# W_base stage of an AdaLN-FFN kernel: product 6 of pairs 2 to 7 as seven inner products for two pairs at once

## The chip, the cores and the metric

One core of one Trainium2 chip (trn2) runs the whole kernel. The metric is the device time of one execution in microseconds, as the median of several runs.

## The reference, cut to what matters

```python
def cond(v, q):                       # v: 16 x 512 x 1024, q: 16 x 512
    q_emb = relu(q @ W3 + b3)
    x = (n * v + sum(v, axis=1)) * q_emb[:, None, :]
    return relu(x @ W2 + b2)          # W2: 1024 x 1024

def ffn(y):
    base = y @ W_base + b_base        # W_base: 1024 x 1024
    shared = (y @ A_s) @ B_s
    gates = top2(softmax(y @ W_router + b_router))
    routed = ((y @ A_r) * gates) @ B_r
    return base + shared + routed

out = x + ffn(cond(x, cond_1024))
```

All in 32-bit floats. The two large products are `@ W2` (stage 1) and `@ W_base` (stage 2), for 16 batches of 512 tokens.

## The kernel before, in words

**Pairs and products.** The 16 batches are worked in 8 pairs, first through stage 1, then, as pairs 0 to 7 again (`g` = 8 to 15, `p = g - 8`), through stage 2. A pair is a 2 x 2 block matrix (two batches, two halves of the 1024 features) and is multiplied by the 2 x 2 blocks of the weight with seven products instead of eight (Strassen's scheme in Winograd's form). The products are numbered 0 to 6; their left operands are the four blocks and four sums of them (`t1` to `t4`). A product has four groups, one for each output tile of 128 features (`j`); a group is 4 chunks (`k`) of 128 x 3 matmuls of 128 x 512. The three stand for one exact one: an operand is split into a high part (ScalarE, `high`, to `act_hi`) and a low part (VectorE, `low`, to `act_lo`), and the helper `three` multiplies high by high, low by high and high by low. A group is 12 matmuls.

**Joined products.** Pairs 2 to 7 of stage 2 are taken two by two: an even one (`even`) and the odd one after it (`odd`). Product 1 of both, and product 4 of both, is again a 2 x 2 block product and is done by seven inner products (`inner`) of 12 matmuls each, all in the even pair. They take their weights from DRAM (`inner_scratch`) to `inner_w` through GpSimd's queue, one step ahead; their operands are `inner_high` and `inner_low` on 1024 columns, with four inner sums (`inner_t1` to `inner_t4`). The other pair's block waits in `partner` or `partner4`. Product 6 is done pair by pair at the pair's end.

**Banks.** Of the 8 PSUM banks, 0 to 3 hold a pair's running sums: product 0 writes them, products 2, 3, 5 and 6 add to them, and between two products an engine takes out what that bank holds then (`copy_p0`, `copy_u2`, `copy_u4` on ScalarE, `c12_bank`, `c22_of`, `c21` on VectorE). Banks 4 to 7 serve the inner products and the low-rank rows of C11.

**Low-rank rows.** `shared` and `routed` are a product of 128 rows (`ha`, `hb`) that is added onto the output tiles: three matmuls a tile, for C12 and C11 as tiles of their own (`low_rank_c12`, `low_rank_c11`), for the rest inside `group` of products 5 and 6.

**What sets the order.** Each engine runs a list that is written out by hand (`even`, `odd`, `before_next` for VectorE; `even`, `odd` for ScalarE and TensorE), strictly in order; semaphores tie the lists. SyncE's queue loads the inputs, intermediate y and x, and stores the outputs. `bank_free` and `inner_free` say what a group waits for before it writes its bank:

```python
                elif n == 5:
                    if four_joined(g):
                        pe.wait_ge(c12_base, base_no(g, j))
...
                else:
                    pe.wait_ge(c22_done, four(g, j))
```

**The end of a pair** is, on TensorE, product 5 (in an even pair with three inner products between its groups) and the four groups of product 6; on VectorE `before_next`: the low part of the next pair's product 0, chunk by chunk, with C21 of this pair (`c21`, line 1841 through `add_bank`) and `t1` of the next (line 1789) between them.

## Time and profile before

| | us |
|---|---|
| median of 3 runs | 1389.74 |
| lowest, highest | 1389.46, 1389.89 |
| the profiled execution's own time | 1388.26 |
| its span | 1386.5 |
| TensorE matmul (PE), weight load (PEld) busy | 1382.0, 1135.4 |
| VectorE (DVE), ScalarE (ACT), GpSimd (POOL) busy | 1037.3, 663.3, 75.2 |
| HBM read, written | 171.69 MB, 82.71 MB |

The span runs from the first to the last instruction of the profiled execution; times in rows count from its start. A matmul's row gives 389 ns, because matmuls overlap: what one costs is the distance between the starts of two. Names in a row read output<-inputs, `xN` is a count, and what stands in brackets is the idle time before the instruction and who ended it. Most lines are those of helpers: 2786 to 2788 are the three matmuls of `three`, 1773 and 2187 the low parts of 512 and 1024 columns, 1841 a bank plus bias plus buffer, 2204 and 2216 a bank plus buffer, 2463 the low-rank rows added to C11, 1789, 1816 and 1837 the sums t1, t3 and t4.

### The profile page before, as it was taken

The page shows a single profiled execution, that of the slowest core. Times are in us where ns is not written, and L with a number is a line of the kernel's source. Part 1 is how long each engine was busy: PE and PEld are TensorE (multiplying, and loading weights), DVE is VectorE, ACT ScalarE, POOL GpSimd, SP SyncE. Part 2 cuts the span into 40 slices and gives each one's busy share as a digit, 9 for nine tenths or more (in the row PEclk, how much of TensorE's full clock was granted, in tenths as well). Part 3 has the DMA queues.
Part 4 walks back from the last instruction along what each step waited for, and adds up shares of the span by engine and source line. Part 5 has one row for each costly group of instructions (what it writes and reads, how often), then busy time and mean ns, then how long its engine had stood idle before and what let it go on. Part 6 is the DMA issues. An engine that isn't in the chain of part 4 may idle for free.

```text
span 1386.5 us, 18363 instructions
## 1 busy us (share of the span) xinstructions
PE 1382.0 (100%) x6069; PEld 1135.4 (82%) x6069; DVE 1037.3 (75%) x1700; ACT 663.3 (48%) x1209; POOL 75.2 (5%) x163
## 2 busy tenths in 40 slices
PE   9999999999999999999999999999999999999999
PEld 5888888888888888888888888888888888888887
DVE  6977777675776757867889768887777876778665
ACT  7774755647556574655554233443224432344231
POOL 2000110000000000000000000110001000010000
PEclk9999999999999999999999999999999999999999
DMA  8253835545165451545836629868575684846734
GB/s 320 66 178 113 264 124 156 176 116 172 62 177 163 120 166 58 158 150 175 293 124 175 240 94 348 312 193 273 179 257 175 203 277 164 280 158 202 241 117 157
DMA packets 151327, 255.63 MB, mean 184 GB/s; under 512 B 40416, under 2 KB 40672, under 8 KB 151232
## 3 DMA queue, kind: packets, MB, share of 16 engines
q1 hardware_dynamic: 135680, 199.75, 44.6%
q0 software_dynamic: 13680, 49.81, 11.7%
q10 hardware_dynamic: 1872, 4.89, 0.9%
q8 instruction: 48, 0.79, 0.2%
q14 instruction: 47, 0.39, 0.1%
HBM read 171.69 MB, written 82.71 MB: 183 GB/s over the span
## 4 chain that ended last, share of the span: by engine, by line
PE 100%; DVE 0%; DVEq 0%; issue 0%
PE ps L2786 33%; PE ps L2787 33%; PE ps L2788 33%; PE ps L2797 1%; PE ps L2812 0%; PE ps L2806 0%; DVE buf L2779 0%; DVEq L59 0%; DVE zeros L1954 0%
## 5 line engine op out<-in xcount | busy, mean ns | idle before, releaser
L2786 PE MATMUL ps<-act_hi,w_hi 128*128 128x512 f32 x1504 | 585.3, 389 | 0.0
L2788 PE MATMUL ps<-act_hi,w_lo 128*128 128x512 f32 x1504 | 585.1, 389 | 0.0
L2787 PE MATMUL ps<-act_lo,w_hi 128*128 128x512 f32 x1504 | 585.1, 389 | 0.0
L2786 PEld LDWEIGHTS ps<-act_hi,w_hi 128*128 128x128 f32 x1504 | 282.3, 188 | 59.6 <-DVE act_lo L1766 0.9
L2788 PEld LDWEIGHTS ps<-act_hi,w_lo 128*128 128x128 f32 x1504 | 282.3, 188 | 58.7
L2787 PEld LDWEIGHTS ps<-act_lo,w_hi 128*128 128x128 f32 x1504 | 282.3, 188 | 58.6
L1011 ACT ACTIVATE act_hi<-src 128x512 fp32r<-128x512 f32 x208 | 124.8, 622 | 95.9 <-PE ps L2788 91.9
L1773 DVE TENSOR_TENSOR act_lo<-src,act_hi 128x512 fp32r<-128x512 f32 x192 | 129.3, 684 | 22.1 <-ACT act_hi L1011 22.1
L1030 ACT ACTIVATE yhi<-buf 128x512 fp32r<-128x512 f32 x128 | 80.2, 626 | 81.1 <-PE ps L2788 80.6
L1841 DVE SCALAR_TENSOR_TENSOR buf<-ps,bb_sb,buf 128x512 f32<-128x512 f32 x91 | 67.2, 746 | 56.3 <-PE ps L2788 54.0
L2786 PE MATMUL ps<-act_hi,inner_w 128*128 128x512 f32 x252 | 98.1, 389 | 0.0
L2788 PE MATMUL ps<-act_hi,inner_w 128*128 128x512 f32 x252 | 98.1, 389 | 0.0
L2787 PE MATMUL ps<-act_lo,inner_w 128*128 128x512 f32 x252 | 98.0, 389 | 0.0
L1841 DVE SCALAR_TENSOR_TENSOR buf<-ps,b_sb,buf 128x512 f32<-128x512 f32 x80 | 59.4, 748 | 43.7 <-PE ps L2788 43.6
L1766 DVE SCALAR_TENSOR_TENSOR act_lo<-src,shift,act_hi 128x512 fp32r<-128x512 f32 x104 | 76.7, 748 | 19.2 <-ACT act_hi L1008 19.2
L1011 ACT ACTIVATE act_hi<-buf 128x512 fp32r<-128x512 f32 x64 | 39.6, 628 | 79.4 <-DVE buf L1806 57.0
L1008 ACT ACTIVATE act_hi<-src,shift 128x512 fp32r<-128x512 f32 x100 | 69.9, 714 | 11.4 <-PE ps L2788 9.4
L1896 DVE TENSOR_TENSOR buf_lo<-buf,yhi 128x512 fp32r<-128x512 f32 x64 | 43.5, 687 | 35.8 <-ACT yhi L1030 35.7
L961 ACT ACTIVATE src<-src,qn 128x512 f32<-128x512 f32 x92 | 65.4, 711 | 4.7 <-DMA src<-in_xT 4.7
L1063 ACT ACTIVATE buf<-ps 128x512 f32<-128x512 f32 x60 | 35.7, 595 | 66.5 <-PE ps L2788 66.5
L1052 ACT ACTIVATE buf<-ps 128x512 f32<-128x512 f32 x64 | 37.2, 591 | 55.8 <-PE ps L2788 55.5
L1773 DVE TENSOR_TENSOR act_lo<-buf,act_hi 128x512 fp32r<-128x512 f32 x64 | 43.1, 687 | 27.3 <-ACT act_hi L1011 27.2
(181 smaller groups left out, 1659.8 us busy)
## 6 DMA issues: line engine op xcount, KB each, us to landing
src<-in_xT SPq DMA_DIRECT2D x224, 256.0 KB, 3.8
y_scratch<-buf SPq DMA_DIRECT2D x128, 256.0 KB, 3.2
src<-y_scratch SPq DMA_DIRECT2D x128, 256.0 KB, 5.3
inner_w<-inner_scratch POOLq DMA_DIRECT2D x63, 512.0 KB, 3.8
outT<-buf SPq DMA_DIRECT2D x115, 256.0 KB, 4.8
inner_scratch<-staged POOLq DMA_DIRECT2D x14, 512.0 KB, 5.1
wl_raw<-in_wbase SPq DMA_DIRECT2D x7, 1024.0 KB, 5.7
partner<-y_scratch POOLq DMA_DIRECT2D x12, 512.0 KB, 5.0
```

What stands on the lines that cost most here:

```text
L961: nc.scalar.activation(src[:, t, :], src[:, t, :], ACT.Identity, scale=qn[:, H * HALF_OF[q] + k, 2 * i + BATCH_OF[q]:2 * i + BATCH_OF[q] + 1],
L1008: nc.scalar.activation(act_hi[:, slot(g, n, k), :], source[:, t, :], ACT.Identity, bias=shift[:, t:t + 1]).then_inc(hi_done, 1)
L1011: nc.scalar.activation(act_hi[:, slot(g, n, k), :], source[:, t, :], func).then_inc(hi_done, 1)
L1030: nc.scalar.activation(yhi[:, (y_no(i, c, j) - 1) % 2, :], buf[:, j, :], func).then_inc(yhi_done, 1)
L1052: nc.scalar.activation(buf2[:, j, :], ps[:, j, :], ACT.Copy).then_inc(u2_copied, 1)
L1766: nc.vector.scalar_tensor_tensor(act_lo[:, s, :], source, shift[:, t:t + 1], act_hi[:, s, :].bitcast(F32), ALU.add, ALU.subtract).then_inc ...
L1773: nc.vector.tensor_tensor(act_lo[:, s, :], source, act_hi[:, s, :].bitcast(F32), ALU.subtract).then_inc(lo_done, 1)
L1841: nc.vector.scalar_tensor_tensor(buf, ps[:, bank, :], bias, buf, ALU.add, ALU.add).then_inc(done, 1)
L1896: nc.vector.tensor_tensor(lo, y, hi, ALU.subtract).then_inc(ylo_done, 1)
L2786: nc.tensor.matmul(out, wh, a_h, start=start, stop=False, skip_group_check=onto)
L2787: nc.tensor.matmul(out, wh, a_l, start=False, stop=False, skip_group_check=onto)
L2788: return nc.tensor.matmul(out, wl, a_h, start=False, stop=stop, skip_group_check=onto)
```

## The change

Product 6 of an even and the odd pair after it becomes seven inner products, like products 1 and 4, but in the odd pair: four stand behind the groups of product 3, three between the groups of product 5. The even pair's operand t4 is kept for them (`keep_t4`, a copy to `partner6` on ScalarE); `inner_tiles` takes the odd pair's t4 as the other. The even pair's C21 is gathered in `acc6` (bank plus bias plus buffer in `c21_of`, then three inner results in `six_add`) and stored in the odd pair. The low-rank rows of product 6 become tiles of their own (`low_rank_d`), the first before the last group of product 5, three behind it. In the first couple of pairs (2 and 3) the seven inner weights are made from a quadrant that is loaded again: seven high parts and seven stores on ScalarE, seven low parts and four sums on VectorE. `before_next` is no longer called for these pairs; low parts, C21 and t1 are written into `even` and `odd`. In `odd` the order of t3, t4 and the low parts changes.

```diff
+            def keep_t4(e):
+
+                g = QUADS[e]
+                for q in range(2):
+                    if e == EARLY:
+                        act.wait_ge(four_stored[q], 16 * four_stores(4, q))
+                    else:
+                        act.wait_ge(inner_done, inner_no(RUN[e - 1, 6], L2 - 1, 1))
+                for h in range(2):
+                    act.wait_ge(t4_made, four(g, 2 * h + 1))
+                    at = slice(tile(G21, 2 * h), tile(G21, 2 * h + 2))
+                    kept = nc.scalar.activation(partner6[:, 2 * h:2 * h + 2, :], src[:, at, :], ACT.Copy)
+                kept.then_inc(a_ready, 1)
...
+            def six_add(e, m, jt):
+
+                r, g = RUN[e, 6], QUADS[e]
+                dve.wait_ge(inner_done, inner_no(r, m, jt))
+                bank = (A_BANKS if m % 2 == 0 else B_BANKS)[jt]
+                if m in (0, 1, 2, 5):
...
+                    nc.vector.tensor_tensor(buf2[:, j, :], ps[:, bank, :], buf2[:, j, :], ALU.add
+                                            ).then_inc(inner_added, 1)
+                elif m == 3:
+                    dve.wait_ge(c21_done, four(g, 2 + jt))
+                    nc.vector.tensor_tensor(acc6[:, 2 + jt, :], ps[:, bank, :], acc6[:, 2 + jt, :], ALU.add
+                                            ).then_inc(inner_added, 1)
+                elif m == 4:
+                    dve.wait_ge(inner_added, added_no(r, SIX_V, jt))
+                    nc.vector.tensor_tensor(acc6[:, 2 + jt, :], ps[:, bank, :], acc6[:, 2 + jt, :], ALU.add
+                                            ).then_inc(c21_out, 1)
+                else:
+                    dve.wait_ge(c21_done, four(g, jt))
+                    nc.vector.tensor_tensor(acc6[:, jt, :], ps[:, bank, :], acc6[:, jt, :], ALU.add
+                                            ).then_inc(c21_out, 1)
+
+            def c21_of(p, j):
+
+                g = NP + p
+                bias = bb_sb[:, H + j:H + j + 1]
+                dve.wait_ge(lr_done, lr_no(p, LR_D, j))
+                if g in QUADS:
+                    dve.wait_ge(x21_added, four(p, H - 1))
+                    dve.wait_ge(buf2_stored[j], 16 * g)
+                    if g == SECOND:
+                        dve.wait_ge(inner_w_lo, 4 * L2)
+                    nc.vector.scalar_tensor_tensor(acc6[:, j, :], ps[:, j, :], bias, buf2[:, j, :], ALU.add, ALU.add
+                                                   ).then_inc(c21_done, 1)
+                else:
+                    f = RUN[QUADS.index(g - 1), 6]
+                    dve.wait_ge(inner_added, added_no(f, SIX_P1, j) if j < 2 else added_no(f, SIX_P6, j - 2))
+                    add_bank(j, bias, buf2[:, j, :], c21_done)
...
+                first = e == EARLY
...
+                if first:
+                    inner_weight_low(3 * L2)
...
+                if first:
+                    inner_weight_low(3 * L2 + 1)
                 inner_low(f, 3)
...
                 add_u2(f, 0)
+                if first:
+                    inner_weight_low(3 * L2 + 2)
+                    inner_weight_sums(3)
                 inner_low(f, 4)
                 low(g, 5, 0)
                 low(g, 5, 1)
...
                 add_u2(f, 1)
                 inner_low(f, 5)
                 u4_add_x(p, 0)
+                if first:
+                    inner_weight_low(3 * L2 + 3)
                 u4_add_x(p, 1)
                 inner_low(f, 6)
+                if first:
+                    inner_weight_low(3 * L2 + 4)
                 add_u4(f, 0)
                 add_u4(f, 1)
                 u4_add_x(p, 2)
                 u4_add_x(p, 3)
                 c22_of(p, 0)
+                lr_low_d(p)
+                if first:
+                    inner_weight_low(3 * L2 + 5)
                 c22_of(p, 1)
                 add_p6(f, 0)
                 add_p6(f, 1)
-                low(g, 6, 0)
-                low(g, 6, 1)
-                lr_low_d(p)
-                c22_of(p, 2)
                 u2_add_x(p, 2)
                 u2_add_x(p, 3)
-                low(g, 6, 2)
-                low(g, 6, 3)
                 u2_add_x(p, 0)
                 u2_add_x(p, 1)
+                low(g + 1, 0, 0)
+                low(g + 1, 0, 1)
+                if first:
+                    inner_weight_low(3 * L2 + 6)
+                c22_of(p, 2)
+                c21_of(p, 0)
+                low(g + 1, 0, 2)
+                low(g + 1, 0, 3)
                 c22_of(p, 3)
+                for j in range(1, H):
+                    c21_of(p, j)
+                    t1(g + 1, j - 1)
+                t1(g + 1, H - 1)
 
...
             def odd(p):
                 g = NP + p
+                e = QUADS.index(g - 1)
+                f = RUN[e, 6]
                 for j in range(H):
                     t2(g, j)
                     if j > 0:
...
                 low(g, 2, H - 1)
                 lr_low_a(p)
                 for j in range(H):
+                    t4(g, j)
                     low(g, 3, j)
-                    t3(g, j)
-                    t4(g, j)
-                    if j == 0:
-                        lr_low_b(p)
                     if j > 0:
                         c11_add_low(p, j - 1)
+                for j in range(H):
+                    t3(g, j)
+                lr_low_b(p)
+                inner_low(f, 0)
+                inner_t1(f)
                 c11_add_low(p, H - 1)
+                inner_low(f, 1)
+                inner_t2(f)
+                u2_add_x(p, 0)
+                u2_add_x(p, 1)
+                six_add(e, 0, 0)
+                six_add(e, 0, 1)
+                inner_low(f, 2)
+                inner_t3(f)
+                c12_bank(p, 0)
+                u2_add_x(p, 2)
+                u2_add_x(p, 3)
+                six_add(e, 1, 0)
+                six_add(e, 1, 1)
+                inner_low(f, 3)
+                inner_t4(f)
+                c12_bank(p, 1)
+                six_add(e, 2, 0)
+                six_add(e, 2, 1)
+                inner_low(f, 4)
+                for j in range(H):
+                    low(g, 5, j)
+                c12_bank(p, 2)
+                six_add(e, 3, 0)
+                six_add(e, 3, 1)
+                inner_low(f, 5)
+                c12_bank(p, 3)
                 for j in range(H):
                     c11_add_x(p, j)
-                    low(g, 5, j)
-                    c12_bank(p, j)
-                for j in range(H):
-                    u4_add_x(p, j)
-                    u2_add_x(p, j)
-                for j in range(H):
-                    low(g, 6, j)
-                    if j == 2:
-                        lr_low_d(p)
+                six_add(e, 4, 0)
+                six_add(e, 4, 1)
+                inner_low(f, 6)
+                u4_add_x(p, 0)
+                u4_add_x(p, 1)
+                lr_low_d(p)
+                c22_of(p, 0)
+                u4_add_x(p, 2)
+                u4_add_x(p, 3)
+                c22_of(p, 1)
+                six_add(e, 5, 0)
+                six_add(e, 5, 1)
+                for j in range(H):
                     c12_add_x(p, j)
-                    if j > 0:
-                        c22_of(p, j - 1)
-                c22_of(p, H - 1)
+                c22_of(p, 2)
+                if p < LAST:
+                    low(g + 1, 0, 0)
+                    low(g + 1, 0, 1)
+                c21_of(p, 0)
+                six_add(e, 6, 0)
+                six_add(e, 6, 1)
+                if p < LAST:
+                    low(g + 1, 0, 2)
+                    low(g + 1, 0, 3)
+                c22_of(p, 3)
+                c21_of(p, 1)
+                c21_of(p, 2)
+                if p < LAST:
+                    t1(g + 1, 0)
+                    c21_of(p, 3)
+                    for j in range(1, H):
+                        t1(g + 1, j)
 
...
-                    if n == 4 or 0 < e < EARLY:
+                    if n == 6:
+                        pe.wait_ge(c11_low, low_no(g + 1 - NP, 2 + jt))
...
+            def low_rank_d(p, j):
+
+                pe.wait_ge(c22_done, four(NP + p, j))
+                if j == 0:
+                    pe.wait_ge(lr_lo_done, 3 * p + 4)
+                cols = slice((H + j) * P, (H + j + 1) * P)
+                three(ps[:, j, :], low_hi[:, cols], low_lo[:, cols], ha_hi[:, :], ha_lo[:, :], False, True,
+                      True).then_inc(lr_done, 1)
+
+            def last_part(g, f):
+                for j in range(H):
+                    group(g, 5, j, (1, 3 * (g - NP) + 3, hb_hi, hb_lo))
+                    if j < H - 1:
+                        inner(f, H + j)
+                    if j == H - 2:
+                        low_rank_d(g - NP, 0)
+                for j in range(1, H):
+                    low_rank_d(g - NP, j)
+
             def even(e):
                 g = QUADS[e]
                 r, f = RUN[e, 1], RUN[e, 4]
...
                 for j in range(H):
                     group(g, 3, j)
                     inner(f, j)
-                for j in range(H):
-                    group(g, 5, j, (1, 3 * (g - NP) + 3, hb_hi, hb_lo))
-                    if j < H - 1:
-                        inner(f, H + j)
+                last_part(g, f)
 
             def odd(p):
                 g = NP + p
+                f = RUN[QUADS.index(g - 1), 6]
                 for j in range(H):
                     group(g, 0, j)
                 for j in range(H):
                     group(g, 2, j)
                     low_rank_c11(p, j)
-                group(g, 3, 0)
-                group(g, 3, 1)
-                low_rank_c12(p, 0)
-                group(g, 3, 2)
-                low_rank_c12(p, 1)
-                group(g, 3, 3)
-                low_rank_c12(p, 2)
-                low_rank_c12(p, 3)
-                for j in range(H):
-                    group(g, 5, j, (1, 3 * p + 3, hb_hi, hb_lo))
+                for j in range(H):
+                    group(g, 3, j)
+                    if j > 0:
+                        low_rank_c12(p, j - 1)
+                    inner(f, j)
+                low_rank_c12(p, H - 1)
+                last_part(g, f)
```

VectorE at the border from an odd pair to an even one (pair 3 to pair 4), before: the low parts of the next product 0 (1773), the four additions that end C21 (1841 into buf2) and t1 (1789), then the first inner low part (2187) and the first inner sum of the even pair.

```order
L1773 TENSOR_TENSOR act_lo<-src,act_hi 128x512
L1841 SCALAR_TENSOR_TENSOR buf2<-ps,bb_sb,buf2 128x512
L1789 TENSOR_TENSOR src<-src 128x512
L1773 TENSOR_TENSOR act_lo<-src,act_hi 128x512
L1841 SCALAR_TENSOR_TENSOR buf2<-ps,bb_sb,buf2 128x512
L1789 TENSOR_TENSOR src<-src 128x512
L1773 TENSOR_TENSOR act_lo<-src,act_hi 128x512
L1841 SCALAR_TENSOR_TENSOR buf2<-ps,bb_sb,buf2 128x512
L1789 TENSOR_TENSOR src<-src 128x512
L1841 SCALAR_TENSOR_TENSOR buf2<-ps,bb_sb,buf2 128x512
L2187 TENSOR_TENSOR act_lo<-src,act_hi 128x1024
L2121 SCALAR_TENSOR_TENSOR partner<-partner,src 128x1024
```

The same place now (1898 was 1773, 1966 was 1841, 1914 was 1789, 2322 was 2187, 2251 was 2121; 2395 is `six_add`).

```order
L1966 SCALAR_TENSOR_TENSOR buf3<-ps,bb_sb,buf3 128x512
L1898 TENSOR_TENSOR act_lo<-src,act_hi 128x512 x2
L1966 SCALAR_TENSOR_TENSOR buf2<-ps,bb_sb,buf2 128x512
L2395 TENSOR_TENSOR acc6<-ps,acc6 128x512 x2
L1898 TENSOR_TENSOR act_lo<-src,act_hi 128x512 x2
L1966 SCALAR_TENSOR_TENSOR buf3<-ps,bb_sb,buf3 128x512
L1966 SCALAR_TENSOR_TENSOR buf2<-ps,bb_sb,buf2 128x512 x2
L1914 TENSOR_TENSOR src<-src 128x512
L1966 SCALAR_TENSOR_TENSOR buf2<-ps,bb_sb,buf2 128x512
L1914 TENSOR_TENSOR src<-src 128x512 x3
L2322 TENSOR_TENSOR act_lo<-src,act_hi 128x1024
L2251 SCALAR_TENSOR_TENSOR partner<-partner,src 128x1024
```

Three t1 now stand together between the last C21 and the first inner low part, and the last C22 (into buf3) stands just before the C21 additions.

VectorE in the even pair 2, between the third inner product's result and the low parts of product 5, before (2216 is the bank addition, 2187 the fifth inner low part, 1773 x4 product 5's):

```order
L2167 SCALAR_TENSOR_TENSOR t2_four<-src,t2_four 128x1024
L1841 SCALAR_TENSOR_TENSOR acc4<-ps,bb_sb,acc4 128x512
L2216 TENSOR_TENSOR acc4<-ps,acc4 128x512
L2187 TENSOR_TENSOR act_lo<-partner4,act_hi 128x1024
L1773 TENSOR_TENSOR act_lo<-src,act_hi 128x512 x4
```

And now:

```order
L2302 SCALAR_TENSOR_TENSOR t2_four<-src,t2_four 128x1024
L1966 SCALAR_TENSOR_TENSOR acc4<-ps,bb_sb,acc4 128x512
L2351 TENSOR_TENSOR acc4<-ps,acc4 128x512
L2186 TENSOR_TENSOR staged_6<-wl_raw,staged_6 128x512
L2204 TENSOR_TENSOR wl_raw<-wl_raw 128x2x256
L2205 TENSOR_TENSOR wl_raw<-wl_raw 128x2x256
L2207 TENSOR_TENSOR wl_raw<-wl_raw 128x2x256
L2209 TENSOR_TENSOR wl_raw<-wl_raw 128x2x256
L2322 TENSOR_TENSOR act_lo<-partner4,act_hi 128x1024
L1898 TENSOR_TENSOR act_lo<-src,act_hi 128x512 x4
```

One low part and the four sums of the weights stand between the same two instructions.

TensorE at the end of a pair now, from the last chunk of product 5's last group on:

```order
L3036 MATMUL ps<-act_hi,w_hi 128x512
L3037 MATMUL ps<-act_lo,w_hi 128x512
L3038 MATMUL ps<-act_hi,w_lo 128x512
L3036 MATMUL ps<-hb_hi,low_hi 128x512
L3037 MATMUL ps<-hb_lo,low_hi 128x512
L3038 MATMUL ps<-hb_hi,low_lo 128x512
L3036 MATMUL ps<-ha_hi,low_hi 128x512
L3037 MATMUL ps<-ha_lo,low_hi 128x512
L3038 MATMUL ps<-ha_hi,low_lo 128x512
```

The last three rows stand three times there, for tiles 1, 2 and 3; before, each was the end of a group of product 6.

## Rows read from the trace of the kernel before

**Rows 1.** The page: busy time of the engines, and the chain that ended last.

```profile
PE 1382.0 (100%) x6069; PEld 1135.4 (82%) x6069; DVE 1037.3 (75%) x1700; ACT 663.3 (48%) x1209; POOL 75.2 (5%) x163
...
PE 100%; DVE 0%; DVEq 0%; issue 0%
```

**Rows 2.** Busy time by pair of stage 2: pair 2, pair 3, pair 4.

```profile
core 0: us, PE busy (x) PEld busy (x) DVE busy (x) ACT busy (x) POOL busy (x), PEclk, DMA share, GB/s
876.06:979.48 103.42, 103.42 (x458) 85.51 (x456) 81.06 (x109) 39.62 (x61) 8.94 (x16) 1.00 0.73 250
979.48:1045.07 65.59, 65.58 (x290) 53.98 (x289) 47.88 (x76) 19.77 (x33) 1.46 (x2) 1.00 0.65 221
1045.07:1148.47 103.40, 103.40 (x457) 85.50 (x456) 79.35 (x106) 38.39 (x57) 8.95 (x16) 1.00 0.65 211
```

**Rows 3.** Timeline of TensorE: start, length; a pair's first matmul, its first inner matmul.

```profile
1045.06 0.39 PE L2786 MATMUL ps<-act_hi,w_hi 128*128 128x512 f32 x1
...
1047.78 0.39 PE L2786 MATMUL ps<-act_hi,inner_w 128*128 128x512 f32 x1
```

**Rows 4.** Timeline of all engines, last C12 tile of pair 3.

```profile
1016.20 0.39 PE L2786 MATMUL ps<-hb_hi,low_hi 128*128 128x512 f32 x1
1016.40 0.60 ACT L1063 ACTIVATE buf<-ps 128x512 f32<-128x512 f32 x1 [2.28 <-PE ps L2788]
...
1017.05 0.50 PE L2786 MATMUL ps<-hb_hi,low_hi 128*128 128x512 f32 x1
...
1017.38 0.39 PE L2787 MATMUL ps<-hb_lo,low_hi 128*128 128x512 f32 x1
```

**Rows 5.** Timeline of VectorE at the border from pair 3 to pair 4.

```profile
1045.33 0.75 DVE L1841 SCALAR_TENSOR_TENSOR buf<-ps,bb_sb,buf 128x512 f32<-128x512 f32 x1 [2.05 <-PE ps L2788]
1046.00 1.22 DVE L2187 TENSOR_TENSOR act_lo<-src,act_hi 128x1024 fp32r<-128x1024 f32 x1
1047.13 1.22 DVE L2121 SCALAR_TENSOR_TENSOR partner<-partner,src 128x1024 f32<-128x1024 f32 x1
```

**Rows 6.** Groups by line: busy us, mean ns of one, idle before.

```profile
L1773 DVE TENSOR_TENSOR act_lo<-src,act_hi 128x512 fp32r<-128x512 f32 x192 | 129.3, 684 | 22.1 <-ACT act_hi L1011 22.1
...
L2187 DVE TENSOR_TENSOR act_lo<-src,act_hi 128x1024 fp32r<-128x1024 f32 x15 | 18.3, 1220 | 5.6 <-ACT act_hi L1283 5.6
...
L2204 DVE TENSOR_TENSOR acc<-ps,acc 128x512 f32<-128x512 f32 x6 | 4.1, 692 | 1.8 <-PE ps L2788 1.8
```

**Rows 7.** Timeline of VectorE and TensorE in pair 2, before product 5.

```profile
936.71 0.75 DVE L1841 SCALAR_TENSOR_TENSOR acc<-ps,bb_sb,acc 128x512 f32<-128x512 f32 x1
937.56 0.69 DVE L2216 TENSOR_TENSOR acc<-ps,acc 128x512 f32<-128x512 f32 x1
938.67 1.23 DVE L2187 TENSOR_TENSOR act_lo<-partner,act_hi 128x1024 fp32r<-128x1024 f32 x1 [0.42 <-ACT act_hi L1283]
939.81 2.50 DVE L1773 TENSOR_TENSOR act_lo<-src,act_hi 128x512 fp32r<-128x512 f32 x4
...
942.76 0.39 PE L2786 MATMUL ps<-act_hi,w_hi 128*128 128x512 f32 x1
```

**Rows 8.** Timeline of VectorE in pair 3: product 3's first low part, last C11 addition.

```profile
992.42 0.68 DVE L1773 TENSOR_TENSOR act_lo<-src,act_hi 128x512 fp32r<-128x512 f32 x1
...
1004.23 0.69 DVE L2463 TENSOR_TENSOR buf<-ps,buf 128x512 f32<-128x512 f32 x1 [1.37 <-PE ps L2788]
```

**Rows 9.** DMA issues: count, KB each, median us to landing.

```profile
inner_scratch<-staged ACTq DMA_DIRECT2D x7, 512.0 KB, 6.3
```

**Rows 10.** The waits: us in total, times, longest.

```profile
ACT staged L1197 <- DMA inner_scratch<-staged: 19.8, 7, 4.9
```

**Rows 11.** DMA from 1360 us on: GB/s in 40 slices, and an issue.

```profile
GB/s 247 232 346 254 164 3 0 365 87 340 0 0 167 229 0 229 387 387 387 374 216 0 263 133 0 0 0 219 176 0 0 0 167 229 0 0 0 249 147 0
...
outT<-buf ACTq DMA_DIRECT2D x1, 128.0 KB, 1.7
```

**Rows 12.** Timeline of TensorE: its last matmul.

```profile
1382.85 0.39 PE L2788 MATMUL ps<-ha_hi,low_lo 128*128 128x512 f32 x1
```

316 lines of the change are left out of this document (227 added, 89 removed).

## The prediction

> **What bounds the kernel now.** I read the page's busy times and chain first. TensorE is busy for 1382.0 of 1386.5 us and the chain that ended last is all TensorE [rows 1]. The windows by pair say the same of the stage that the change touches [rows 2]: an even pair takes 103.42 us, an odd pair 65.59 us, and TensorE is busy all that time at a granted clock of 1.00, its 2.4 GHz level. Consecutive matmuls start 0.2267 us apart: 12 of them lie between 1045.06 and 1047.78 [rows 3]. 744 matmuls in an even and an odd pair make 168.7 us of the 169.0 measured. So every matmul left out is worth a pitch, and every microsecond that TensorE waits is lost, since no later slack absorbs it. The other thing to see is VectorE: 47.88 of 65.59 us busy in an odd pair, 79 to 81 of 103.42 in an even one [rows 2]. It runs its list in order, so what counts is the moment at which it reaches an instruction that TensorE needs.
>
> LDWEIGHTS fill only 82% of the span [rows 1], and the constant pitch says that this is no headroom. The Trainium skill (Perfetto Trace Analysis, Identifying the Most-Contended Engine) says to judge TensorE by LDWEIGHTS busy and not by matmul busy, which would leave it 18% of slack; that reading is a rival below.
>
> **The matmuls.** Product 6 of two pairs was 2 x 4 tiles x 12 = 96 matmuls; seven inner products of 12 are 84. The low-rank rows (3 matmuls a tile) stay as many. 12 fewer for each of three couples of pairs, 36 in all, x 0.2267 = **8.16 us less**. The Trainium skill (TensorE: Matmul & The Clock Gate, Wait — 56ns, not 53.3ns?) gives 512 columns / 2.4 GHz + 2.5 ns = 215.7 ns, by which the 36 would be worth 7.77 us, an estimate from that page; the trace shows 0.2267 and decides.
>
> **A wait that goes.** In each odd pair ScalarE's copy of bank 3 of product 3 starts 0.20 us after that group's end (1016.20) and ends at 1017.00; the low-rank tile that waits for it goes on at 1017.05 and its next matmul at 1017.38, 0.28 us late [rows 4]. Now an inner product stands between group and tile. 3 x 0.28 = **0.84 less**. The same rows price a handover: TensorE's stream resumes 0.16 us after the end of the instruction that it waits for. VectorE starts 0.27 us after the end of a group whose last matmuls are low-rank ones (the group ended at 1045.06, the addition began at 1045.33 [rows 5]).
>
> **VectorE in an odd pair.** Added are seven low parts and four sums on 1024 columns (1.22 us [rows 6]) and 14 additions from banks (0.69); gone are four low parts (0.68): 13.4 + 9.7 - 2.7 = 20.4 us. 68.3 us of work then stand in 324 x 0.2267 = 73.4 us. That fits, with 5 us to spare, and only if nothing is late. In a queue one instruction follows another after 0.60 us (four take 2.50 [rows 7]), an addition from a bank with bias after 0.67, one on 1024 columns after 1.13 [rows 5]; one that reads the result just before it, after 0.85 [rows 7]. With these I laid VectorE's new list against TensorE's, 0 being the pair's first matmul. I speak only of the places with under 1 us left.
>
> (a) *First inner product of product 6.* VectorE comes to the sums t4 at 12.94, as before (992.42 [rows 8] less 979.48). The C11 rows of tile 2 end at 21.08, so their addition starts at 21.35; after it 0.60, four t3 2.40, the two low-rank instructions 0.72 + 0.61, the first inner low part 1.13 and the first inner sum 1.13 bring the addition of tile 3 to 27.94, its end to 28.63 and TensorE to 28.79. In the trace of before this addition had nobody behind it (1004.23 [rows 8]); now the second half of the inner product writes its bank and is due at 27.20 + 1.36 = 28.56. **0.25 us in each of three odd pairs, 0.75 more.**
>
> (b) *The end of a pair.* Behind product 5's last tile (end 71.40) stand three low-rank tiles, ending at 72.08, 72.76 and 73.44. The last needs VectorE's C22 of tile 3: 71.67 + 0.75 + 0.16 = 72.58, due 72.76: covered, with 0.18 to spare. Then VectorE has C21 of tile 1 at 72.35, of tile 2 at 73.03, t1 at 73.70, C21 of tile 3 at 74.30 and three more t1 from 74.97 to 76.77; only then comes the first inner low part of the even pair, ready at 77.99 and used at 78.15. TensorE wants it one group after the pair's start, 73.44 + 2.72 = 76.16. Before, it began 0.94 us after the border [rows 5] and was ready 0.5 us early. **2.0 us at each of two borders (odd to even), 4.0 more.** From even to odd the same crowd costs nothing: there a whole product 0 follows, whose next operands are late only by some 2 us in 10.9.
>
> (c) *The couple that makes the weights (pair 2).* Seven low parts (0.68) and four sums of weights come into VectorE's list and ScalarE waits for its own stores, 6.3 us to landing [rows 9]. In VectorE's list the bank addition of the third inner product gives way at 938.16 (937.56 + 0.60); a weight part and four sums follow, three of them bound to the result before them: 0.85 + 0.60 + 0.85 + 0.85 + 0.60 = 3.75 us. The fifth inner low part then starts at 941.91 instead of 938.67, product 5's first low part at 943.04; it is ready at 943.72 and used at 943.88, where TensorE wants it at 942.76 [rows 7]. **1.1 more, once.** ScalarE's second weight part waits until 934.9 for a landing and frees product 3's bank 0.7 us later than before, which VectorE does not feel. The later stores fall into waits for TensorE; the copy of product 6's operands then starts some 3 us after the border and its readers come 10 us later.
>
> (d) *The end.* Before, the final half tile was stored behind one store in 3.4 us. Now four stores of 256 KB become ready in 1.6 us and SyncE issues one in 0.5. A half store lands after 1.7 us, 0.34 of it transfer at the highest rate of the last stretch, 387 GB/s [rows 11]; so 1.3 MB that begin at 72.7 are through after 1.3 + 3.4 us, at 77.4. The span of before ended 3.4 us after TensorE's last slot (1382.85 + 0.23 [rows 12]), which is 76.9 here. **0.5 more** (bounds 0 and 1.5).
>
> Costs nothing: 21 more loads of inner weights on GpSimd's queue (each has over 8 us between the product that frees its buffer and the one that reads it), and the four y loads that now wait for ScalarE's copy.
>
> **The sum.** -8.16 - 0.84 + 0.75 + 4.0 + 1.1 + 0.5 = -2.65 us. The profiled execution took 1388.26 us, which becomes 1385.6; it stands 1.5 us below the median of the runs, 1389.74, which becomes **1387.1**. The bounds of what before does not show: at best the waits (a) to (d) are covered, -9.0 in all; at worst VectorE's idle time of before stays, see the second rival.
>
> **Rivals.** *All covered:* TensorE waits nowhere. For it speaks that 5 us of VectorE are free and that each wait is a difference of small numbers; against it the order of (b), where three t1 stand in front of the low part whatever else happens. 1389.7 - 9.0 = 1380.7, up to 1382 with (a) or (c) left. 0.12.
>
> *VectorE becomes the bound of the odd pair,* the slower side. An odd pair of before has 65.59 - 47.88 = 17.7 us of VectorE idle, waits for results of TensorE. If half of them stay beside 68.3 us of work, an odd pair takes 77.2 us instead of 73.4, 3.8 us more in each of three, 11.4 in all: 1398.5. It decides from 0.9 us per odd pair on (2.65 / 3). The place would be product 5 with its inner products. Against it: between 35 and 68 us VectorE meets a result of TensorE every 3 to 6 us and by my list is never more than 1 us behind. 0.09.
>
> *ScalarE's stores in pair 2 come late:* one landing waited out in front of a part of product 5 or of a copy adds up to 6.3 us, 1389 to 1393. For it: ScalarE waited up to 4.9 us for such landings when weights were made before, 7 times [rows 10]. 0.06, half of it within 0.2%.
>
> *The matmuls were no bound* (the reading by LDWEIGHTS): 36 fewer give nothing, and the added waits of 6.35 us remain: 1396.1. The constant pitch speaks against it. 0.02.
>
> That the change does not do what it says is out: the built lists hold 36 matmuls fewer.
>
> **How the numbers follow.** About 0.2%, 2.8 us, can be told from no change by a measurement of this kernel, and my forecast (0.71; its own range 1385.0 to 1389.5) lies at that bound: 0.32 of it on the faster side, 0.39 inside. Faster: 0.32 + 0.12 = 0.44. Within: 0.39 + 0.03 = 0.42. Slower: 0.09 + 0.03 + 0.02 = 0.14. The range 1381.5 to 1391.5 leaves out half of the first rival, the second and the last: 0.17.
>
> **What would show it.** In the profile after: 6033 matmuls; pairs 2 to 7 at 92.5 and 73.4 us plus waits; at the starts of pairs 4 and 6 a gap of 2 us before the first matmul with inner_w, released by VectorE's low part; a gap of 1.1 us before product 5 of pair 2; no gap before the last C12 tile of odd pairs; VectorE about 68 us busy in an odd pair. Wrong would be a gap inside an odd pair's second half, or no gap at the starts of pairs 4 and 6.

## The result, and the profile after

The changed kernel takes **1400.44 us** (median of 4 runs, 1400.20 to 1400.78), the kernel before 1389.60 beside it (4 runs, 1388.22 to 1389.89): ratio 1.008, 95% interval 1.0064 to 1.0096. It is slower; 1387.1 was forecast, and the range ended at 1391.5. The profiled execution's span is 1398.8 us against 1386.5, 12.3 more.

The page of the kernel after, where [rows 1] stood for before: busy times, and the chain that ended last.

```profile
PE 1378.9 (99%) x6033; PEld 1129.0 (81%) x6033; DVE 1090.1 (78%) x1762; ACT 681.2 (49%) x1219; POOL 86.4 (6%) x184
...
PE 85%; DMA 5%; DVE 4%; SPq 3%; issue 2%; ACT 1%; DVEq 0%; ACTq 0%
PE ps L3036 28%; PE ps L3038 28%; PE ps L3037 28%; DMA ha_raw<-hw_scratch 2%; SPq L515 1%; DMA inner_scratch<-staged 1%; DMA outT<-buf 1%; PE ps L3047 1%; DMA buf<-in_xT 1%; DVE buf L1966 1%; DVE act_lo L1898 0%; DVE staged L2186 0%; DVE buf L2652 0%; SPq L853 0%; DMA gates_scratch<-wtok 0%
```

36 matmuls are gone, as counted. But the chain is no longer all TensorE: 5% are transfers, the load of ha_raw ahead of all. Busy time by pair of stage 2, pairs 2 to 7 (columns as in [rows 2]):

```profile
876.91:972.67 95.76, 93.42 (x409) 76.27 (x408) 82.73 (x114) 42.84 (x65) 7.88 (x14) 1.00 0.82 286
972.67:1046.79 74.12, 74.01 (x326) 60.66 (x325) 66.52 (x98) 27.57 (x39) 6.25 (x11) 1.00 0.66 216
1046.79:1146.00 99.21, 94.57 (x409) 77.39 (x408) 76.38 (x103) 37.02 (x55) 8.89 (x16) 0.98 0.75 253
1146.00:1221.33 75.33, 73.99 (x325) 60.65 (x324) 66.32 (x98) 25.60 (x37) 5.20 (x9) 1.00 0.61 201
1221.33:1320.60 99.27, 93.52 (x410) 76.27 (x408) 76.30 (x103) 37.15 (x55) 8.90 (x16) 1.00 0.73 250
1320.60:1394.09 73.49, 73.49 (x325) 60.55 (x323) 63.83 (x94) 20.42 (x30) 2.65 (x5) 1.00 0.52 175
```

Without a wait an even pair is 92.5 us and an odd one 73.4. Pairs 3 and 5 are 0.7 and 1.9 us over that (VectorE is busy in them for 66.5 and 66.3, 68.3 forecast), pair 2 is 3.3 over, and the even pairs 4 and 6 are 6.7 and 6.8 over. The waits of pair 4, up to 1066 us (us in total, times, longest):

```profile
ACT ha_hi L1612 <- DMA ha_raw<-hw_scratch: 13.5, 1, 13.5
DVE buf L2277 <- DMA outT<-buf: 8.3, 1, 8.3
...
PE ps L3036 <- DVE ha_lo L2624: 2.6, 1, 2.6
...
PE ps L3036 <- DVE act_lo L2322: 2.1, 1, 2.1
```

The last row is the wait of step (b), 2.1 us. The others are new: ScalarE stands 13.5 us in front of the copy of ha_raw, VectorE 8.3 us in front of the inner sum t2 (`inner_t2`), whose buffer buf2 is still being stored, and TensorE loses 2.6 us at the low-rank rows that read ha_lo. Why these transfers are late stands in SyncE's queue. Its issues in the kernel after, around the border from pair 5 to pair 6 (1221.33), with start and length; it was idle until the first row, where it waited 30.3 us for VectorE's C11 addition:

```profile
1198.42 0.34 SPq L810 DMA_DIRECT2D outT<-buf  x1
...
1202.35 6.16 SPq L814 DMA_DIRECT2D buf<-in_xT  x4
1208.61 6.30 SPq L515 DMA_DIRECT2D src<-y_scratch  x12
1214.96 1.84 SPq L834 DMA_DIRECT2D outT<-buf  x4
1216.90 3.11 SPq L515 DMA_DIRECT2D src<-y_scratch  x4
1220.07 2.35 SPq L764 DMA_DIRECT2D outT<-acc  x2
...
1226.07 3.92 SPq L853 DMA_DIRECT2D outT<-buf  x4
1230.08 1.08 SPq L691 DMA_DIRECT2D ha_raw<-hw_scratch  x1
```

The same queue before, border at 1214.06:

```profile
1174.54 0.34 SPq L758 DMA_DIRECT2D outT<-buf  x1
...
1190.36 4.76 SPq L471 DMA_DIRECT2D src<-y_scratch  x8
...
1215.53 0.38 SPq L647 DMA_DIRECT2D ha_raw<-hw_scratch  x1
```

Before, the first C11 store leaves 40 us ahead of the border and ha_raw 1.5 us behind it. Now the first C11 store leaves 23 us ahead, nearly everything behind it is issued without a pause (SyncE waits 3.4 us in all, for stores of buf1, within the four loads at 1202.35), and ha_raw leaves 8.75 us behind the border. The diff moves the odd pair's four `c11_add_x` behind the additions of the first four inner results of product 6 (`six_add`); SyncE's stores of C11 wait for them, and all its other work stands behind these stores. The transfers then collide. DMA from 1204 to 1244 us, after (GB/s in 40 slices, the total, and issues with KB and us to landing), then before:

```profile
GB/s 363 326 338 371 307 197 246 385 389 399 416 397 393 397 410 373 365 367 404 397 408 402 385 404 404 406 408 404 404 408 420 397 383 404 402 395 160 78 20 106
DMA packets 7089, 14.03 MB, mean 351 GB/s; under 512 B 789, under 2 KB 789, under 8 KB 7086
...
outT<-buf SPq DMA_DIRECT2D x12, 256.0 KB, 9.4
...
ha_raw<-hw_scratch SPq DMA_DIRECT2D x1, 256.0 KB, 8.8
```

```profile
DMA packets 3688, 7.90 MB, mean 198 GB/s; under 512 B 409, under 2 KB 409, under 8 KB 3686
...
outT<-buf SPq DMA_DIRECT2D x8, 256.0 KB, 5.4
...
ha_raw<-hw_scratch SPq DMA_DIRECT2D x1, 256.0 KB, 2.6
```

**Theory 1:** the place of the C11 additions in VectorE's list holds SyncE's queue, and its transfers come late and bunched. **Theory 2:** VectorE has too much to do in the odd pair (the second rival of the prediction, 1398.5 us). **Theory 3:** the added bytes themselves fill the DMA engines. A fourth reading, that matmuls are no bound, is tried at the end.

### The profile page after: what moved, and what is told of

Same layout as the page of the kernel before. It is cut to its first block, busy times and chain, and to the rows that moved or that the text cites. A ratio compares the mean times of both kernels' runs of the same rounds, so it can differ in the third digit from the quotient of the medians.

```text
span 1398.8 us, 18472 instructions
## 1 busy us (share of the span) xinstructions
PE 1378.9 (99%) x6033; PEld 1129.0 (81%) x6033; DVE 1090.1 (78%) x1762; ACT 681.2 (49%) x1219; POOL 86.4 (6%) x184
## 4 chain that ended last, share of the span: by engine, by line
PE 85%; DMA 5%; DVE 4%; SPq 3%; issue 2%; ACT 1%; DVEq 0%; ACTq 0%
PE ps L3036 28%; PE ps L3038 28%; PE ps L3037 28%; DMA ha_raw<-hw_scratch 2%; SPq L515 1%; DMA inner_scratch<-staged 1%; DMA outT<-buf 1%; PE ps L3047 1%; DMA buf<-in_xT 1%; DVE buf L1966 1%; DVE act_lo L1898 0%; DVE staged L2186 0%; DVE buf L2652 0%; SPq L853 0%; DMA gates_scratch<-wtok 0%
## 5 line engine op out<-in xcount | busy, mean ns | idle before, releaser
L3036 PE MATMUL ps<-act_hi,w_hi 128*128 128x512 f32 x1408 | 548.2, 389 | 0.8 <-DVE act_lo L1898 0.8
L3038 PE MATMUL ps<-act_hi,w_lo 128*128 128x512 f32 x1408 | 547.8, 389 | 0.0
L3037 PE MATMUL ps<-act_lo,w_hi 128*128 128x512 f32 x1408 | 547.7, 389 | 0.0
L3036 PEld LDWEIGHTS ps<-act_hi,w_hi 128*128 128x128 f32 x1408 | 264.4, 188 | 57.1 <-issue 1.2
L3038 PEld LDWEIGHTS ps<-act_hi,w_lo 128*128 128x128 f32 x1408 | 264.3, 188 | 54.9
L3036 PE MATMUL ps<-act_hi,inner_w 128*128 128x512 f32 x336 | 131.8, 392 | 6.3 <-DVE act_lo L2322 6.3
L3038 PE MATMUL ps<-act_hi,inner_w 128*128 128x512 f32 x336 | 130.8, 389 | 0.0
L3037 PE MATMUL ps<-act_lo,inner_w 128*128 128x512 f32 x336 | 130.8, 389 | 0.0
L3036 PEld LDWEIGHTS ps<-act_hi,inner_w 128*128 128x128 f32 x336 | 63.0, 188 | 23.0 <-DVE act_lo L2322 9.0
L929 POOL DMA_DIRECT2D inner_w<-inner_scratch x84 | 45.0, 537 | 576.1 <-PE ps L3038 544.5
L3038 PEld LDWEIGHTS ps<-act_hi,inner_w 128*128 128x128 f32 x336 | 63.1, 188 | 13.3
L3037 PEld LDWEIGHTS ps<-act_lo,inner_w 128*128 128x128 f32 x336 | 63.1, 188 | 12.8
```

The costliest lines, as they stand in the source:

```text
L929: pool.dma_start(inner_w[:, c % 2], inner_dram[kind, m]).then_inc(inner_w_loaded[c % 2], 16)
L3036: nc.tensor.matmul(out, wh, a_h, start=start, stop=False, skip_group_check=onto)
L3037: nc.tensor.matmul(out, wh, a_l, start=False, stop=False, skip_group_check=onto)
L3038: return nc.tensor.matmul(out, wl, a_h, start=False, stop=stop, skip_group_check=onto)
```

## The experiments

Each ran 4 to 12 times beside the kernel before (medians of 1388.7 to 1388.9 in these runs, 1389.6 beside the changed kernel). "Less" and "more" are against the changed kernel's 1400.44 where nothing else is named, and since the kernel before differs by 0.9 us from group to group, differences under 1 us between experiments say nothing.

**1. The C11 additions early again.** In `odd(p)` of VectorE:

```diff
                 u2_add_x(p, 1)
+                c11_add_x(p, 0)
+                c11_add_x(p, 1)
                 six_add(e, 0, 0)
...
                 c12_bank(p, 0)
+                c11_add_x(p, 2)
+                c11_add_x(p, 3)
                 u2_add_x(p, 2)
...
                 c12_bank(p, 3)
-                for j in range(H):
-                    c11_add_x(p, j)
                 six_add(e, 4, 0)
```

> The changed kernel with the odd pair's four additions of C11 back near the places they had before (tiles 0 and 1 behind product 2's addition of tile 1, tiles 2 and 3 behind the C12 rows of tile 0). Theory 1, SyncE's queue stands behind the late C11 stores and its transfers bunch at the border: the first C11 stores leave about 13 us earlier, the waits of 2.7 to 3.2 us on the high part of the next pair's operands, the slow matmuls behind them, the 1.1 us before the third inner product and the 1.5 us at the last low-rank tile go: 4.2 + 3.6 + 1.1 + 1.5 = 10 us less, about 1390. Theory 2, VectorE has too much to do in the odd pair: the additions are the same work at another place, so at most 1 us changes, 1399.5 to 1402. Theory 3, the added bytes alone (the stores of two half tiles more at the border) fill the DMA engines: about half of the 10 us goes, 1395.

1389.21 us, 11.2 less (ratio to before 1.000, 0.9991 to 1.001). Pairs 3 to 6 of its profile:

```profile
973.36:1047.08 73.72, 73.72 (x325) 60.76 (x324) 66.00 (x98) 27.80 (x39) 6.25 (x11) 1.00 0.76 249
1047.08:1141.65 94.57, 92.87 (x409) 76.43 (x408) 76.15 (x103) 36.69 (x54) 8.89 (x16) 1.00 0.72 243
1141.65:1215.37 73.72, 73.72 (x325) 60.75 (x324) 66.00 (x98) 25.79 (x37) 5.20 (x9) 1.00 0.71 233
1215.37:1309.90 94.53, 92.83 (x409) 76.42 (x408) 76.55 (x103) 36.67 (x54) 8.90 (x16) 1.00 0.71 241
```

VectorE does the same 66.0 us of work in an odd pair, and the pair takes 73.72: theory 2 falls. What is left over 92.5 and 73.4 in these pairs is what the prediction had: 1.86 + 0.11 us at each odd-to-even border (b) and 0.25 in each odd pair (a). Pair 2 is not in this: it takes 97.15 us, 4.6 over and 1.4 more than in the changed kernel, with waits for ha_lo and before the third inner product. DMA moves nearly the same bytes around the border (20.24 MB between 1166 and 1246 us, 20.53 in the changed kernel), and theory 3 expected only half the gain: the added bytes alone are not the cause.

**2. The three last t1 behind the inner low parts.** They leave the end of `odd` and stand in the next `even`:

```diff
                 inner_low(r, 1)
+                for j in range(1, H if e > EARLY else 0):
+                    t1(g, j)
                 inner_t2(r)
```

> The changed kernel with the three last sums t1 of an odd pair made behind the first two inner low parts of the next even pair, so that the first inner low part follows C21 of tile 3 at once. The wait of 2.0 to 2.2 us before the first inner product of pairs 4 and 6 goes in both theories. Theory 1: the wait on the high part of the next operands ends with a landing, at a fixed time, so TensorE only waits that much longer there: 0 to 1 us less in all. Theory 2 (VectorE sets the pace of the border): both stay gained, 4 us less, 1396.4.

1402.17 us, **1.7 more**, a miss: the wait at the borders went (0.17 + 0.11 us left), yet the low-rank rows of the first inner product now waited 4.24 and 4.89 us instead of 2.73 and 3.19, and behind both waits the clock fell (last section). TensorE came earlier to a landing that did not (it went on 18.2 and 18.8 us behind the border, 18.7 and 19.0 in the changed kernel): a wait that ends with a transfer cannot be shortened by being early.

**3. Both edits.**

> Both edits together. Theory 1: 10 us from the queue and now also the 4.2 us of the sums, since no landing waits behind them: about 1386. Theory 2: as with the sums alone, 1396.

1386.85 us (0.9975 to 0.9999 of before). With the landings gone the same t1 edit is worth 2.4 us, of the 4.2 expected; that the sum comes near the 1386 expected is in part luck, since the first edit gave 11.2 and not 10. The 12 runs lie between 1383.85 and 1391.12, and in the profiled one pair 6 still lost 0.6 us for ha_raw and 1.2 behind it: the load is only just in time.

**4. The C11 additions late in the kernel before.**

```diff
                 for j in range(H):
-                    c11_add_x(p, j)
                     low(g, 5, j)
                     c12_bank(p, j)
+                for j in range(H):
+                    c11_add_x(p, j)
```

> The kernel before, with only the odd pair's four additions of C11 moved behind product 5's operands and the C12 rows, so that their stores leave some 15 us later; nothing of the joined product 6 is in it. Theory 1: the transfers bunch here too, but this kernel has 6 MB less to move in the 40 us around the border, so 0 to 3 us more than before, with the load of the next pair's operands landing later. Theory 2: 0. If it is slower by 8 us or more, the place of the additions alone explains the whole result, whatever the joined product adds.

1396.43 us, 7.5 more than the kernel before (ratio 1.005, 1.0038 to 1.0062), a miss by size. The next pair was not longer (pair 4 took 103.47 us; only pair 2, 104.63, was). The loss is inside the odd pairs, 68.37, 68.65 and 67.47 us instead of 65.59. VectorE of pair 5 in this kernel, with its wait and what ended it, and TensorE behind it:

```profile
1196.67 0.69 DVE L2505 TENSOR_TENSOR buf<-src,buf 128x512 f32<-128x512 f32 x1 [1.84 <-DMA src<-in_xT]
...
1199.68 0.69 DVE L2505 TENSOR_TENSOR buf<-src,buf 128x512 f32<-128x512 f32 x1 [1.72 <-DMA src<-in_xT]
```

```profile
1206.63 0.50 PE L2787 MATMUL ps<-act_hi,w_hi 128*128 128x512 f32 x1 [1.74 <-DVE buf L1841]
...
1209.69 0.50 PE L2787 MATMUL ps<-act_hi,w_hi 128*128 128x512 f32 x1 [0.72 <-DVE act_lo L1773]
```

The loads of x that the U4 addition reads alternate with the C11 stores in SyncE's queue and went late with them. So one moved block of four 0.6-us additions costs 7.5 us here and 11.2 in the changed kernel, through two different readers of the same queue. This is theory 1, by a path I had not thought of. How much of the 3.7 us between the two is due to the bytes that the change adds is not shown.

**5. ha_raw of even pairs issued by ScalarE,** the C11 additions left late:

```diff
                 inner_high(r, 1)
+                d_rows_used(act, p - 1)
+                act.wait_ge(hw_stored[GA], 16 * (p + 1))
+                act.dma_start(ha_raw[:], hw_dram[2 * p]).then_inc(ha_loaded, 16)
```

> The changed kernel (C11 additions late, as it has them) with only the next even pair's load of ha_raw issued by ScalarE, right behind its copy of the second inner product's operands, instead of by SyncE behind all stores of the odd pair. Theory 1a, the wait is SyncE's order: the load leaves some 7 us earlier (1222 instead of 1230 in pair 6), lands before its copy is due even if it takes the 8.8 us it took, and the waits of 2.7 to 3.2 us with the slow matmuls behind them and the wait before the third inner product go: 8 to 9 us less, 1392. Theory 1b, the DMA engines are full and any transfer lands at the end of the backlog (1238), whoever issues it: 0 to 1 us less, 1399.5. Theory 2, VectorE: 0.

1395.53 us: 4.9 less, between 1a and 1b. The load left at 1217.7 us, 0.2 behind the border, and landed in 5.6 us, not 8.8, although the engines were as full (share 1.06, 398 GB/s from 1216 to 1222). SyncE's loads of the same size, issued in the same stretch of this run (1210 to 1225 us), took nearly twice as long (KB and median us to landing last):

```profile
src<-y_scratch SPq DMA_DIRECT2D x6, 256.0 KB, 10.5
...
ha_raw<-hw_scratch ACTq DMA_DIRECT2D x1, 256.0 KB, 5.6
```

So part of the 8.8 us is what stands ahead in SyncE's own queue. The Trainium skill (DMA: Bandwidth & Descriptors, Queues, rings and completion order) says that SP and ACT each own one row of rings and that a DMA engine takes turns between the rows it has work for; the shorter landing agrees. The gain stopped at the next landing. Waits up to 1063 us in pair 4 of this kernel:

```profile
DVE buf L2279 <- DMA outT<-buf: 9.0, 1, 9.0
...
ACT ha_hi L1611 <- DMA ha_raw<-hw_scratch: 2.1, 1, 2.1
PE ps L3038 <- DVE act_lo L2324: 2.0, 1, 2.0
PE ps L3038 <- DVE ha_lo L2626: 1.9, 1, 1.9
```

ha_hi was ready, but VectorE stood 9.0 us in front of t2, waiting for the store of C21, with ha_lo behind it in its list.

**6. As 5, and t2 in a buffer that is not being stored** (t2_four for buf2 in the first inner run of even pairs from pair 2 on, and no wait for buf2_stored ahead of it):

```diff
+                if RUNS[r][0] >= EARLY:
+                    t2_half = t2_four[:]
...
-                if n == 1:
+                if n == 1 and e < EARLY:
                     buf2_free(e, (0, 1))
```

> The changed kernel, C11 additions late, with ha_raw from ScalarE and, of even pairs, the sum t2 of the first inner run in the buffer t2_four instead of buf2, so that it no longer waits for the stores of C21 tiles 0 and 1. With ha_raw alone VectorE stood 9.0 us in front of t2 until 1060.6 for such a store, and ha_lo behind it was late again. Theory 1: the second landing was what took the place of the first; pair 4 loses its 2.1 us and the slow matmuls behind them (1.8), pair 6 its 1.2 us before the third inner product: 4 to 5 us under that run's 1395.5, 1390.5 to 1391.5. Rival: there is a third wait behind it (the store of C21 tile 2 before t3, or a C22 store before ScalarE's copy): less than 1.5 us gained, 1394 to 1395.5.

1392.24 us (1390.55 to 1395.26): 3.3 less than 5, and just short of the 4 to 5 expected. No low-rank rows wait for ha_lo now. With VectorE's order untouched 8.2 of the 11.2 us are back. The profiled execution is the slowest of the eleven; what is left in it beside (a) to (c) are 1.28 and 2.34 us at the last low-rank tile of pairs 3 and 5, behind late y loads, slow matmuls behind the second, 0.8 us at a group of pair 6, and 1.0 and 1.3 us before the third inner product of pairs 4 and 6.

**7. The y loads ahead of the C11 stores in SyncE's queue,** VectorE's list untouched: in odd pairs the loads of G11 and G21 (eight `load_y`, with their waits) are moved to here from behind the loads of buf1:

```diff
+                if more and four_joined(g):
+                    for k in range(H):
+                        sp.wait_ge(lo_done, op_no(g, 5, k))
+                        load_y(p + 1, G11, k)
...
                 for j in range(H):
                     sp.wait_ge(c11_out, four(p, j))
```

> The changed kernel with VectorE's order untouched; in SyncE's queue the eight loads of the next pair's y (groups G11 and G21) of an odd pair stand in front of the four C11 stores instead of behind them. SyncE idles until 1198.4 for the first C11 addition, and these loads are ready some 4 to 8 us earlier. Theory 1: eight issues of 0.5 us and 2 MB leave the backlog, so ha_raw and the stores of C21 leave about 4 us earlier: 4 to 8 us less, 1392 to 1396. Theory 2: the same VectorE list, so 0, 1400.4.

1395.48 us, 5.0 less. No engine but SyncE has another order, so the loss is in the queue: the third thing against theory 2. ha_raw left 5.9 us behind the border of pair 6 instead of 8.75, and TensorE no longer waited for it in pairs 4 and 6. The waits at the last low-rank tile of pairs 3 and 5 stayed (2.2 and 1.6 us).

**8. Only half of the C11 additions early** (tiles 0 and 1 as in 1, tiles 2 and 3 as in the change):

```diff
                 u2_add_x(p, 1)
+                c11_add_x(p, 0)
+                c11_add_x(p, 1)
...
-                for j in range(H):
+                for j in (2, 3):
                     c11_add_x(p, j)
```

> The changed kernel with only tiles 0 and 1 of the odd pair's C11 additions early, tiles 2 and 3 late. Theory 1, SyncE's queue in order: four of its DMAs leave early, all others still stand behind the store of tile 2 until 1198, so 2 of 32 us of issue leave the backlog: 1 to 4 us less, 1396.5 to 1399.5. If what counted were the bunching of VectorE's own work behind the sixth additions, half the additions moved would give half of the 11.2 us of all four, 1394.8.

1393.42 us: 7.0 less, more than half of the 11.2 and far more than the 1 to 4 us of my count: a miss. It lies nearer the 1394.8 of the rival, that the bunching of VectorE's own work counts, and this run alone does not refute it. Experiments 5, 6 and 7 do for most of the loss, since they gained 4.9, 8.2 and 5.0 us and left VectorE's order as it was. ha_raw left 5.3 us behind the border of pair 6. That took the waits at the last low-rank tile to nothing (1.61 us in pair 5) and the waits for ha_lo from 2.73 to 0.72 in pair 4 and from 3.19 to 1.82 in pair 6, with the slow matmuls behind the first. The profiled execution is the slowest of the five, 2.3 us above the median. My reading is that a few microseconds less of backlog are enough to clear several of these waits at once; no run tests that by itself.

**9. Edits 1, 2 and 5 together.**

> C11 additions early, the three t1 behind the inner low parts, and ha_raw from ScalarE. With the first two alone the profiled run still waited 0.6 us for ha_raw and 1.2 us before the third inner product in pair 6, 1.0 us at the third inner product of pair 2, and single runs lay between 1383.9 and 1391.1. Theory 1: these go and the runs lie closer together, 1384 to 1385. If the spread has another cause than this load, it stays some 7 us wide.

1383.65 us (0.9957 to 0.998 of before), runs from 1382.9 to 1386.86. The profiled run has no wait in pairs 4 to 7 but (a) and 0.16 us at the borders. Its pair 2 fell to 93.61 us from 95.47 in experiment 3, from which it differs by ha_raw alone: that load no longer stands behind the C21 stores and the 1 MB of weights in SyncE's queue. It moved 21.83 MB between 1166 and 1246 us (20.53 in the changed kernel) without those waits, so theory 3 falls.

**10. Four edits more:** wl_raw[:, 6] loaded behind `load_x12`; in pair 2 `inner_weight_sums(3)` behind `add_u2(f, 1)` instead of ahead of `inner_low(f, 4)`; in odd pairs `c11_add_low(p, H - 1)` ahead of `inner_t1(f)`; C21 stores of tiles 0 and 2 of the last pair from ScalarE. Of these:

```diff
                 load_x12(p)
+                if g == SECOND:
+                    sp.wait_ge(bank_done, group_no(g - 1, 6, H - 1))
+                    load_quadrant(wl_raw[:, 6], Q22, wl_loaded[6])
...
                     inner_weight_low(3 * L2 + 2)
-                    inner_weight_sums(3)
                 inner_low(f, 4)
...
                 inner_low(f, 0)
-                inner_t1(f)
                 c11_add_low(p, H - 1)
+                inner_t1(f)
```

> The three edits and four more: in pair 2 the 1 MB of raw weights behind the other loads and the four sums of weights behind product 5's low parts (the wait of 1.0 us before product 5 goes), in odd pairs the last addition of C11's low-rank rows before the sum t1 (0.25 us in each of three), and at the end two of the C21 stores issued by ScalarE (0 to 0.5 us). TensorE's own time from pair 2 on is 3 x (92.5 + 73.4) = 497.8 us after 876.1; with a tail of 4.3 the span is 1378.2 to 1379, the time 1380 to 1382: faster than the kernel before by 7 to 9 us, which is what its 36 fewer matmuls (8.2 us) and the C12 wait (0.8 us) are worth. If TensorE's matmuls were no bound, it would stay at 1386 or above.

**1380.82 us**, 0.995 of before (0.9937 to 0.9962). Its pairs 2 to 7:

```profile
876.07:969.40 93.33, 93.08 (x410) 76.35 (x409) 82.44 (x114) 42.81 (x65) 7.88 (x14) 1.00 0.83 290
969.40:1042.84 73.44, 73.44 (x326) 60.81 (x325) 65.97 (x98) 27.79 (x39) 6.25 (x11) 1.00 0.77 252
1042.84:1135.60 92.76, 92.76 (x410) 76.43 (x409) 76.02 (x103) 36.74 (x54) 8.89 (x16) 1.00 0.73 246
1135.60:1209.03 73.43, 73.43 (x325) 60.81 (x324) 65.96 (x98) 25.79 (x37) 5.20 (x9) 1.00 0.71 232
1209.03:1301.79 92.76, 92.76 (x409) 76.43 (x408) 76.02 (x103) 36.71 (x54) 8.90 (x16) 1.00 0.74 248
1301.79:1375.23 73.44, 73.44 (x325) 60.62 (x323) 63.58 (x94) 20.41 (x30) 2.65 (x5) 1.00 0.53 180
```

499.2 us where before took 507.0 (from 876.06 to 1382.85 + 0.23): 7.8 less. That is 8.16 for the matmuls and 0.84 for the C12 waits, less 1.2 of small waits that are left (0.3 of them in pair 2, at the inner product behind product 5's first group). Matmuls are the bound, and LDWEIGHTS at 82% of the span was no headroom: the last rival falls.

**11. As 10, with t2 in t2_four.**

> The version with all six edits, plus t2 in t2_four. In its profile no wait for a store is left at the borders of pairs 4 and 6 (0.16 us each, for VectorE's first inner low part), so by theory 1 the median stays at 1380.8 within 0.5 us and only the slowest runs (1383.3) come down.

1380.83 us (0.9931 to 0.9956), five runs from 1380.31 to 1381.16. (The expectations call experiment 10 "all six edits" and this one "all seven edits".) The waits of steps (a) and (c) are gone. Before the first inner product of pair 2 TensorE waits 0.8 us, 0.4 in experiment 10; why is open.

**12. As 11, with the C11 additions late again,** the diff of 1 taken back alone.

> The version with all seven edits, with one taken back: the odd pair's C11 additions late again. The next pair's operands and t2 no longer stand behind SyncE's backlog; the y loads of the odd pair's own end and the stores of C22 and C21 tiles 2 and 3 still do. Theory 1: the waits that were left with ha_raw and t2 freed come back and no others: 1.2 to 2.3 us at the last low-rank tile of pairs 3 and 5, 1 to 2 us before the third inner product of pairs 4 and 6: 5 to 8 us over the seven edits' 1380.8, 1386 to 1389. Theory 2 (VectorE's load, not its order): 0, 1380.8.

1389.83 us (1.0002 to 1.002 of before), 9.0 more than 11 and just over the 5 to 8 expected. Its profiled execution took 1388.12, 1.7 less than the median. So the order of four additions is worth 9 us even where ha_raw and t2 are out of its reach. In pairs 4 and 6 TensorE waits at a group that reads w_hi just ahead of the third inner product (1.6 and 1.4 us) and at that product (1.2 and 1.2), in pair 4 also 0.8 at an inner product ahead of these, and 0.8 at the last low-rank tile of pair 5. That no others would come was wrong: the expectation named neither the w_hi group nor the inner product ahead of it. VectorE again stands 6.6 us for a C21 store, now at t3, whose half of buf2 is still being stored.

## Why the prediction was wrong

The step that failed is the list headed **Costs nothing** and the part on VectorE above it. I walked VectorE's and TensorE's lists and left SyncE's out. The four C11 additions that the diff puts behind product 6's additions occur in no step: their time is in VectorE's list, but what waits for them was put at nothing, the C11 stores and all that stands behind those in SyncE's queue. I took every later landing as in the trace of before. What the runs showed in its place: ha_raw leaves 8.75 us behind the border instead of 1.5 and lands in 8.8 us instead of 2.6, and the place of those four additions alone is worth 11.2 us (experiment 1).

Term by term, forecast against the profile after (TensorE's gaps over its pitch):

| term | forecast, us | measured, us |
|---|---|---|
| 36 matmuls and C12 tiles | -9.0 | as forecast (experiment 10) |
| (a) first inner product of product 6 | +0.75 | 3 x 0.25 = +0.75 |
| (b) two odd-to-even borders | +4.0 | 2.34 + 2.08 = +4.4 |
| (c) pair 2 before product 5 | +1.1 | 0.96 + 0.08 = +1.0 |
| (d) the end, from the last matmul's start | +0.5 | 4.7 - 3.6 = +1.1 |
| pairs 4 and 6: ha_lo, slow matmuls, third inner product | 0 | 4.3 + 4.7 = +9.0 |
| pairs 3 and 5: last low-rank tile | 0 | 0.4 + 1.6 = +2.0 |
| pair 2: first and third inner product | 0 | 0.6 + 1.5 = +2.1 |
| stage 1, up to pair 2 | 0 | +0.8 |
| sum | -2.65 | +12.2 (span +12.3) |

- The matmuls, the waits (a) to (c) and the C12 waits were right to a few tenths, the first and third inner product of pair 2 aside. (d) is at the upper side of its bounds, 0 and 1.5; with two stores on ScalarE, experiment 10's tail was 4.0 us instead of 4.7.
- The missing term is 11 to 13 us: 11.2 by taking the C11 order back (experiment 1). Pair 2's part is another omission of the same kind: 1 MB of weights that the change puts ahead of ha_raw in SyncE's queue. In pair 2 of experiment 9, with ha_raw out of that queue, its two waits were gone; the weights were not moved alone, and the smaller of the two came back in experiments 10 and 11.
- The rival "VectorE becomes the bound" gave 1398.5, near the 1400.4 measured, and was false: VectorE's work in an odd pair is the same in the changed kernel and in experiment 1, 11 us faster. A near number does not confirm a mechanism.
- VectorE's work in an odd pair was forecast at 68.3 us and is 66.3 to 66.5. I added the full durations of instructions that overlap. With the distances between starts that the prediction itself reads (1.13 and 0.60 us) the sum is 47.88 + 11 x 1.13 + 10 x 0.60 = 66.3. So the second rival began from a load 2 us too high.
- I had written that a gap inside an odd pair's second half would show me wrong. It was there, at the last low-rank tile.
- My first wording of theory 1 was too narrow as well. It named one reader, ha_raw; experiments 4, 5, 6 and 12 each found the next one: the x loads, t2, the y loads, t3. That the transfers they wait for stand behind the C11 stores in SyncE's queue is what the edits show; the share of each in the 11.2 us is not shown.

What stays open: how much of the 8.8 us to landing is SyncE's own queue and how much the full engines (5.6 us on ScalarE's queue against 10.5 on SyncE's, in experiment 5, is the nearest measure of it), and the 0.8 us of stage 1, which is within what single profiles differ by (pair 2 began between 875.25 and 876.92 in all of them).

## What to carry to other kernels

When a diff moves an instruction in a compute engine's list, follow what waits for it into the DMA-issuing queue, and walk that queue to the next stage's first load: a queue that waits in order turns one late producer into a late everything. Work that is hidden is hidden only at the place where it stands; here four additions of 0.6 us were worth 11 us by their order alone. If the wait that an edit removes stands in front of one that ends with a landing, price the edit only together with the landing: the same three t1 cost 1.7 us with the backlog and gained 2.4 without it.
